# Weight splitting of seven slots moved from GpSimd to ScalarE, GpSimd keeping the low parts

## The reference, cut to what matters

```python
xn = _layernorm(x)
x = x + _L0_gnn_ref(xn, edge_index, W, b) + _L0_mix_ref(xn[None], W_qkv, gamma, beta, W_out, b_out)[0]
# in _L0_gnn_ref:  h = xn @ W.T + b ; out = segment_sum(norm * h[col], row)
# in _L0_mix_ref:  out = relu-attention(qkv) ; normed = layernorm(out) * gamma + beta ; normed @ W_out + b_out
x = x + _L0_ffn_ref(_layernorm(x)[None], ...)[0]
xn = _layernorm(x)
x = x + _L1_gnn_ref(...) + _L1_mix_ref(...)[0]
x = x + _L1_ffn_ref(_layernorm(x)[None], ...)[0]
```

## Time and profile before

| what | value |
|---|---|
| time, median of 3 runs | 2320.53 us (2320.47 to 2321.92) |
| the profiled execution's own time | 2323.56 us |
| its span, first to last instruction | 2321.7 us |
| PE busy | 2105.8 us (91%) |
| DVE busy | 1262.9 us (54%) |
| ACT busy | 720.1 us (31%) |
| POOL busy | 1136.6 us (49%) |
| mean granted TensorE clock | 0.954 |

### The profile page before, as it was taken

One profiled execution on the slowest core, in us unless ns is written; L12 is line 12 of the kernel. 1 busy time (PEld: TensorE's weight loads), 2 busy tenths in 40 slices (PEclk: granted clock), 3 DMA queues, 4 the chain that ended last, 5 costly groups with the idle time before them and its releaser, 6 DMA issues.

```text
span 2321.7 us, 41575 instructions
## 1 busy us (share of the span) xinstructions
PE 2105.8 (91%) x16528; PEld 1444.8 (62%) x16528; DVE 1262.9 (54%) x2218; ACT 720.1 (31%) x1076; POOL 1136.6 (49%) x811
## 2 busy tenths in 40 slices
PE   6979999999999789879999989979999999985997
PEld 5536564474458666644445567746787788874765
DVE  5882454435678589984633632444544544175332
ACT  4243554535642223330031412311121122051332
POOL 6457778778867422005611773023422524522654
PEclk9989999999999889989999999989999999987999
DMA  3311332242453210032100012300010000366886
GB/s 134 85 29 38 83 91 45 69 109 63 126 122 123 91 53 19 19 130 72 37 1 28 21 44 73 95 28 28 30 53 27 27 19 28 115 258 220 151 151 110
DMA packets 106983, 176.90 MB, mean 76 GB/s; under 512 B 31057, under 2 KB 76248, under 8 KB 100542
## 3 DMA queue, kind: packets, MB, share of 16 engines
q1 hardware_dynamic: 89966, 145.63, 20.0%
q0 software_dynamic: 16848, 28.90, 7.5%
HBM read 120.82 MB, written 53.49 MB: 75 GB/s over the span
## 4 chain that ended last, share of the span: by engine, by line
PE 73%; DVE 12%; POOL 5%; issue 5%; ACT 2%; DMA 2%; DVEq 0%; SPq 0%; POOLq 0%; ACTq 0%
PE ps L481 17%; PE ps L483 17%; PE ps L484 17%; PE pt L691 5%; PE ps L675 3%; DVE RB L772 2%; DVE SR L1735 2%; DVE SR L1877 1%; PE pt L869 1%; DVE RB L1735 1%; PE pt L675 1%; PE ps L1114 1%; PE ps L1115 1%; PE ps L1116 1%; PE pt L1095 1%
## 5 line engine op out<-in xcount | busy, mean ns | idle before, releaser
L481 PE MATMUL ps<-WR,RB 128*128 128x256 f16 (+2 forms) x2280 | 645.7, 283 | 30.4 <-DVE SR L1735 23.8
L483 PE MATMUL ps<-WR,RB 128*128 128x256 f16 (+2 forms) x2280 | 644.8, 283 | 0.0
L484 PE MATMUL ps<-WR,RB 128*128 128x256 f16 (+2 forms) x2280 | 644.2, 283 | 0.0
L1389 POOL TENSOR_TENSOR WR<-WR,units 128x2048 f32<-128x2048 f32 (+2 forms) x25 | 106.9, 4274 | 444.3 <-PE ps L481 421.2
L481 PEld LDWEIGHTS ps<-WR,RB 128*128 128x128 f16 x2280 | 225.6, 99 | 81.3 <-issue 16.0
L481 PE MATMUL ps<-RB,WR 128*128 128x512 f16 (+1 forms) x720 | 246.7, 343 | 9.5 <-DVE RB L433 7.4
L484 PEld LDWEIGHTS ps<-WR,RB 128*128 128x128 f16 x2280 | 225.5, 99 | 45.3 <-issue 0.8
L483 PEld LDWEIGHTS ps<-WR,RB 128*128 128x128 f16 x2280 | 225.8, 99 | 43.0 <-issue 0.8
L483 PE MATMUL ps<-RB,WR 128*128 128x512 f16 (+1 forms) x720 | 246.4, 342 | 0.0
L484 PE MATMUL ps<-RB,WR 128*128 128x512 f16 (+1 forms) x720 | 246.3, 342 | 0.0
L1456 POOL DMA_INDIRECT edges_sorted<-SR x160 | 189.1, 1182 | 72.6 <-issue 56.0
(11 more groups left out here) (336 smaller groups left out, 4020.7 us busy)
## 6 DMA issues: line engine op xcount, KB each, us to landing
WR<-in_w_moe SPq DMA_DIRECT2D x64, 256.0 KB, 3.6
moe_split<-WR SPq DMA_DIRECT2D x128, 128.0 KB, 1.8
RB<-moe_split SPq DMA_DIRECT2D x8, 2048.0 KB, 13.2
WR<-in_w_mix SPq DMA_DIRECT2D x12, 1024.0 KB
WR<-in_w_mix SPq DMA_DIRECT2D x8, 1536.0 KB
RB<-in_x SPq DMA_DIRECT2D x18, 512.0 KB, 6.6
WR<-in_w_out SPq DMA_DIRECT2D x8, 1024.0 KB
RB<-counts SPq DMA_DIRECT2D x10, 640.0 KB, 4.8
```

Source lines behind the costliest of these rows:

```text
L481: m = nc.tensor.matmul(o, ah, bh, start=(k == 0), stop=False)
L483: nc.tensor.matmul(o, ah, bl, start=False, stop=False)
L484: m = nc.tensor.matmul(o, al, bh, start=False, stop=(k == n - 1))
L1389: ch.link(g.tensor_tensor(w, w, units[:, 2:3].to_broadcast([128, width]), ALU.mult))
```

## The change

ACT calls `weights_high` for slots 13 to 19: slot 13 after the first two norm tiles, slots 14, 15, 16 at the end of norm tiles 2, 5 and 7, and slots 17, 18, 19 after its copies of steps 2, 27 and 52. POOL does only `low_part`: slot 13 behind `gain(1)`, slots 14, 15, 16 behind `gain(4)`, `gain(7)` and `gain(9)`, slots 17 to 19 where their splits stood. Loads, products and sizes are the same.

```diff
@@ ScalarE @@
             for i in range(2):
                 norm(i)
+            weights_high(act, 13)
             for i in range(NT):
                 for u in range(4 * i, 4 * i + 4):
                     g_high(u)
@@
                 if i + 2 < NT:
                     norm(i + 2)
+                if i in (2, 5, 7):
+                    weights_high(act, 14 + i // 3)
@@
                 nc.scalar.activation(rw[st % 4], pb[st % 3][0:TN, 0:BW], ACT.Copy).then_inc(rows_out, 1)
+                if st - 1 in (OUTS_AT[0], OUTS_AT[NT], OUTS_AT[2 * NT]):
+                    weights_high(act, 17 + OUTS_AT.index(st - 1) // NT)
@@ GpSimd @@
             gain(1)
+            low_part(13)
             for i in range(2, NT):
-                if i % 2 == 0:
-                    n = SLOT0["gnn0"] + i // 2
-                    split(n, n % 2, 2048)
                 scale(i)
                 gain(i)
+                if i in (4, 7, 9):
+                    low_part(13 + i // 3)
             pool.wait_ge(mm_done, TILE0["mix0_out"])
             pool.wait_ge(z_ready, Z0["lnO"] + NT)
             g.memset(Bc[:, NT:NB].rearrange("p a b -> p (a b)").bitcast(F32), 0.0).then_inc(bc_clear, 1)
-            split(17, 1, 2048)
-            for n in (18, 19):
-                split(n, n % 2, 2048)
+            for n in (17, 18, 19):
+                low_part(n)
```

## The result

The changed kernel takes **2281.22 us** (median of 3 runs, 2280.19 to 2282.31) against 2320.53: the ratio is 0.9828, 95% interval 0.9814 to 0.9842, a gain of 39.3 us; the interval of the ratio stands for 36.7 to 43.2 us. Forecast were 2281 us and a gain of 40. The profiled execution took 2280.19 us on a span of 2278.4, 43.3 less than the span of before.

What follows compares the result with a forecast made beforehand. PE, busy 91% of the span, was taken as the bound, stopped by POOL's splits delaying norm scales and holding DVE. Gains 25.7 + 13.3 + 1 = 40 us from 2320.5 gave 2280.5, stated as 2281 us; range 2272 to 2297.

Steps and rivals of the forecast that it cites:

- Graph product stage, 25.7 us: Slots 13 to 16: PE no longer waits, so the last transposes end at 791.7 instead of 817.4, gaining 25.7 us.
- the sum: Graph product stage from tile 1 without waits: 32 units of 2.62 us plus 9 tiles of 0.87, 91.7 us.
- The margin of 1.7 us at tile 1: Graph product stage: DVE finishes tile 1 near 698.3, 1.7 us before PE asks, so the 3.21 us wait goes.
- Edge stage, 17.3 - 4 = 13.3 us: Steps 23 to 93: old splits of slots 18 and 19 cost 17.3 us; 2 us lost for each remain, gain 13.3.
- PE's three steps in hand: Edge stage: PE's PSUM ring of three steps, 4.8 us, beside which ACT's pair of 3.8 us runs.
- Slot 17, 1 us: Start of the edge stage: low part holds the first add 4.1 us; gain 1 us, at most 4.8.
- A: Rival: PE's waits return in the graph product stage, 3 x 4 us plus low clock; time 2296.5, chance 0.12.
- D: Rival: ACT reaches weights_high before the load lands, holding g_high and norms; slower than before, above 2325 us, chance 0.03.
- B: Rival: edge stage gains nothing, pair and low part, 7.9 us, both on PE's path; time 2294, chance 0.13.
- PE's ring: Edge stage: PSUM ring of three steps, 4.8 us, argued against B because ACT's 3.8 us runs beside it.

Runs made afterwards that it cites:

- the graph part alone: Changed kernel with slots 17 to 19 split whole on POOL again, only slots 13 to 16 changed: 2308.04 us, ratio 0.9890 to before.
- the repetition of the change: The changed kernel itself, unaltered, measured again on another chip beside the margin runs: 2307.09 us, ratio 0.9837 to the kernel before.
- the edge part alone: Changed kernel with slots 13 to 16 as before the change, only slots 17 to 19 changed: 2318.49 us, ratio 0.9935 to before.
- the kernels with slot 17 moved: Changed kernel with ACT making slot 17's pair before step 0: ratio 0.9820; with DVE also making low parts of slots 18 and 19: 0.9794, repeated 0.9803.
- the kernel with the places only: Against before: POOL splits slots 13 to 16 whole, but behind gain(1), gain(4), gain(7), gain(9); slots 17 to 19 as before: 2318.09 us, ratio 0.9933.

## Why the prediction was right

*Graph product stage, 25.7 us.* From tile 1 on, its old wait of 3.21 us included, the traces give 113.32 + 3.21 - 90.88 = 25.65 us, as the sum said: 11.35 us a tile and no wait. At slots 14 to 16 the steps hold one by one: the pairs of 3.8 us, the low part of 4.1, one held `g_low` for each slot, and margins of 2.9 and 3.6 us at tiles 4 and 7. The whole stage gained 27.2 us in the trace of the change, 23.4 in the traces of the two parts on one chip (128.61 - 105.19), and 25.5 by the medians of the graph part alone. The difference lies ahead of where the sum began. After the wait of 3.3 us for tile 0, tile 1 followed 13.23 us later before (without its own wait), 11.64 in this execution of the change and 14.36 in that of the graph part alone, with the granted clock at 1.00 and at 0.79 (a row of each below). I had begun behind it, so this never entered the sum. The margin of 1.7 us at tile 1 also hangs on that clock. In the repetition of the change, at a clock of 0.79, DVE finished tile 1 some 2.8 us before its transposes; at the full clock it finished 0.06 us before them, and they came 11.64 us behind those of tile 0, 0.3 more than PE needs. So tile 1 was the tightest place of the stage.

*Edge stage, 17.3 - 4 = 13.3 us.* Measured 13.6; the edge part alone gained 15.1 by its medians, slot 17 included. The total of 4 us lost was right (3.7), its inside was not. I put ACT's pair at nothing, because it would run beside PE's three steps in hand, and the low part at 2 us a slot. PE's waits say 0.9 us a slot for the pair, and 0.4 and 1.0 for the two low parts; DVE's own low parts, which take the second away, gained 1.7 us for both. That the two errors cancel is luck. The Trainium skill (SBUF — State Buffer, Who interferes with whom) says that the engine which issues first holds the shared ports for its whole instruction, and this trace agrees for DVE: its adds were held 3.78 us by low parts of 4.07. It did not follow that PE pays for all of a hold. One low part for a slot left it a wait of 0.4 or 1.0 us, while a second one, with no work in hand left to hide it, cost it the whole length.

*Slot 17, 1 us.* Measured 1.25 in the trace and 0.7 in the repetition. I put the low part on the first add. In the repetition it held the add of step 1, for 4.01 us, close to that. In the first execution it fell on the one-hot rows of steps 4 and 5, for 5.06 us, just as the old split had the earlier trace rows, and what was gained is the rest of the old split around it. So the place changes from one execution to the next, and the gain hardly.

*The rivals.* A came in no wait between 685 and 791, but its argument, that three tiles carry more than the margins hold, was closer than its 0.12 said: 3.8 us more of ACT's work for each slot bring a first wait of that kind. D's mechanism is real, and one norm tile of earlier placement is enough for one instance of it. B, that pair and low part both fall on PE's path in full, did not come. But its argument against itself, that the pair runs beside PE's ring, was not wholly right: the pair costs PE 0.9 us each time.

That the median came out within 1 us of the forecast is closer than the case can carry. The interval is 3 us wide to either side, and the clock behind the one wait for tile 0 moves an execution by as much.

## What to carry to other kernels

Where a large piece of side work stands in an engine's list ahead of a small step that others wait for, there are two remedies, and each cures what the other leaves. Moving it behind that step helped where its input came late (slot 16: 11.6 us to nothing, while the faster engine in the old place left 12.6). The faster engine helped where the place could not change or the work was too long for it (slots 13 and 15). Of a hold that is about as long as the work in hand, less than half was paid; of a second one behind it, all. And where two new pieces of work stand in a row, price both: the one that I had put at nothing cost as much as the other. Margins found for one delay don't add: the next one is read with the first still being worked off. And where a wait is removed and the time stays, look for the wait that now ends last: here it was a load behind an engine that had been idle anyway.

## What was not expected of the hardware

The granted clock behind one and the same wait differs from execution to execution. The stretch from tile 0 to tile 1 of the change, and of the graph part alone, whose instruction lists are alike there:

```profile
685.36:697.00 11.64, 11.58 (x105) 10.21 (x105) 10.33 (x15) 4.83 (x7) 7.52 (x6) 1.00 0.30 54
```

```profile
699.60:713.96 14.36, 14.36 (x104) 12.23 (x105) 12.82 (x17) 5.62 (x9) 9.87 (x7) 0.79 0.31 75
```

Both follow a wait of 3.3 us, and one lost 2.7 us more by its clock. Of the eleven traces whose lists are alike up to there, two took 11.64 us (1.00), seven 12.93 to 13.08 (0.87 or 0.88), and two 14.36 and 14.37 (0.79). It is not the chip: on one and the same chip the repetition of the change took 14.37 and three others 13.03 to 13.07. Terms under 3 us for a single wait can't be read from one execution. What sets the difference was not tried.

POOL's clearing of the counts, which reads nothing, held an instruction of DVE, as it seems: four one-hot rows that take 1.25 us alone took 2.81 beside its end, in the kernel before, in the change and in the kernels with slot 17 moved. DVE's instruction just ahead of them (a TENSOR_TENSOR with both inputs in SBUF), which also ran beside the clearing, took its usual 0.68 us. In the kernel with the places only, the clearing ended at 818.53, just as the same four rows began, and they were not held:

```profile
818.53 1.26 DVE L1876 TENSOR_SCALAR SR<-SR 128x625 f16<-128x625 f16 x4
```

DVE's own clearing took 5.39 us with and without the low part of POOL beside it. That an instruction which only writes can hold the other engine was seen at this place alone, and no run was made to test it.

The kernel before took 2320.5, 2321.4, 2333.5, 2335.0 and 2347.2 us on the chips used, while the ratio of the change was 0.9828 and 0.9837.
